# Both halves of each weight block kept in a DRAM scratch and loaded as one pair, two raw buffers, a one-function seed for the norms' reciprocal root

## The chip, the core and the metric

The kernel runs on one core of one Trainium2 chip. The metric is the device time of one execution in microseconds. The engines in the rows are PE (TensorE, matmuls), PEld (its weight loads), DVE (VectorE), ACT (ScalarE), POOL (GpSimd) and SP (SyncE), which here issues all DMAs.

## The reference

One block of a network: a state-space scan and a gated feed-forward, each behind a layer norm whose output is scaled and shifted by vectors made from a conditioning input. The input is (1, 2048, 1024) in fp32.

```python
mod = (silu(c) @ wmod).reshape(1, 6, 1, -1)        # sa, ca, ga, sb, cb, gb; ga and gb kept at least 0.25 from zero
h = layernorm(x) * (1 + ca) + sa
xp = h @ x_proj_w.T                                # 32 columns for dt, 16 for B, 16 for C
dt = softplus(xp[..., :32] @ dt_proj_w.T + dt_proj_b)
for t in range(2048):                              # 1024 channels x 16 states
    s = exp(dt[t] * A) * s + dt[t] * B[t] * h[t]
    y[t] = (s * C[t]).sum(states)
x = x + ga * (y + D * h)
h = layernorm(x) * (1 + cb) + sb
gate = h @ gate_w.T + (h @ gate_a.T) @ gate_b.T    # 1024 -> 2752, rank 16
up   = h @ up_w.T   + (h @ up_a.T) @ up_b.T
hidden = silu(gate) * up
out  = hidden @ down_w.T + (hidden @ down_a.T) @ down_b.T
return x + gb * out
```

## The kernel before

**Tiling.** Channels lie on the 128 partitions, tokens on the free axis. The 2048 tokens are cut into six chunks of 256, 320, 368, 368, 368 and 368 (`CH`). The feed-forward of one chunk is a *pass* of `NU` = 72 *units*: one `lora_a`, 44 `gate` and `up` units (25 matmuls each), three `lora_down` and 24 `down` units (21 or 24 matmuls each), in three parts of the hidden dimension. In the first two parts one more `gate` and `up` pair stands between the last hidden tile that `lora_down` needs and `lora_down` itself; in the third it follows directly on the last `up`. A unit needs one block of weights, of up to 128 x 1152 fp32.

**Split products.** Every fp32 product is made of three matmuls in the fast format fp32r: weight high x input high, weight high x input low, weight low x input high. So each block exists as a high half (`whi`, the rounded copy) and a low half (`wlo`, the difference).

**Where the halves come from.** Of 72 blocks, 48 (`PREP`) are prepared before the first pass, between the first scans: SP loads the raw block (`load_prep`), ACT rounds it (`hi_part`, L852, and L854 for the low-rank rows), POOL subtracts (L1267), and SP stores the low half to `lo_scratch` in DRAM (`store_prep`, L526). The high half is thrown away. The other 24 (`OTF`, every third unit) are done in the first pass (POOL L1297, `store_otf` L531). In every pass SP loads for each unit the raw block (`load_raw`, L550) and the low half (`load_lo`, L566), and ACT makes the high half again (`split_hi`, L990), two units ahead of PE. There are three buffers each for `raw`, `whi` and `wlo`: `load_raw(g + 4)` waits for the split of unit g + 1, and `load_lo(g + 3)` for the end of unit g on PE.

**What runs beside it.** During the pass of chunk c the scans of chunk c + 1 run, in 64 *groups* of two channel tiles and one state. For a group ACT makes the decays (exp, L831) and keeps the last state (`hst`, L848), DVE forms the input (L1053) and scans (L1168, two), POOL multiplies by C (L1284) and adds to y (L1257). Groups and the pieces of the norms are dealt out over the units by `pieces_at`, from weights in a table. Each engine has a queue in program order, and all walk through the same list of units: DVE and ACT take the results of unit g - 1 (`used`, `before`, `after`) between the pieces of units g and g + 1. A *head* norm opens the scans of a chunk, a *tail* norm (`TAIL_AT`) its feed-forward: squares are summed on PE, ACT computes a seed of the reciprocal root as exp(-0.5 ln(v)) (L890, L892, piece `rstd`), DVE sharpens it in four steps (L1118 to L1124), DVE multiplies (L1128), and ACT scales and shifts (L909, L910); POOL makes the low half `xlo` (L1275), for which `lora_a` waits.

**The end of the hidden loop.** `hhi` and `hlo` are the halves of the hidden tile: DVE L1191, ACT L1009, POOL L1305. `lora_down` waits for the last `hlo` of its part before its first matmul.

**SP at the start of a pass.** In program order: the last output store of the chunk before (L570), then `load_x` (L536, 1.47 MB), which waits until that chunk's outputs have landed, then the weight loads.

## Time and profile before

| | us |
|---|---|
| median of 3 runs (lowest, highest) | 2398.21 (2397.32, 2401.29) |
| profiled execution | 2402.57 |
| its span, first to last instruction | 2400.6 |
| preparation and scans of the first chunk, up to | 388 |
| passes, from one `lora_a` result to the next | 388 to 736, 1085, 1445, 1807, 2109, end |

The boundaries of the passes are the starts of the six instructions L997, which read the `lora_a` result (388.32, 736.32, 1085.54, 1445.08, 1806.87 and 2109.07 us). A matmul's record is longer than its turn on the engine, since matmuls are pipelined; the pace is read from starts. The profile's page gives over the whole span PE 87% busy, POOL 64%, DVE 60%, ACT 60%, and the DMA queue 68%. These are averages over stages with different limits, so the rows below go by stage. A row of the view by stage has the stretch, its length, busy us (instructions) of PE, PEld, DVE, ACT and POOL, the granted clock as a share of 2.4 GHz, the DMA share and GB/s. "issue" in a bracket stands for idle time for which the profile shows no releaser.

### The profile page before, as it was taken

To read this page: it belongs to the slowest core of one execution; us is meant where nothing else is said; L and a number is where in the kernel's file an instruction comes from. 1 tells how busy PE (TensorE), PEld (TensorE's weight loads), DVE (VectorE), ACT (ScalarE), POOL (GpSimd) and SP (SyncE) were. 2 spreads that over 40 slices of the span, in tenths; PEclk is the share of its full clock that TensorE was granted. 3 is DMA by queue.
4 is the path that set the end of the run, shared out by engine and by line. 5 is a ranking of instruction groups with operands and counts; after the bars stand their busy time and mean duration, and the time that the engine had idled before them with its cause. 6 is when DMAs were issued, how large, how long until landed. Compare 5 with 4: busy or idle time off the path is not lost.

```text
span 2400.6 us, 34580 instructions
## 1 busy us (share of the span) xinstructions
PE 2085.1 (87%) x11700; PEld 1888.9 (79%) x11700; DVE 1446.0 (60%) x2118; ACT 1430.1 (60%) x2798; POOL 1545.0 (64%) x960
## 2 busy tenths in 40 slices
PE   6587754877778989979999989999989999999999
PEld 3243334877767888868999978999979999999998
DVE  4665676767665688755778756678757775211111
ACT  3776766767655677665676655676656565532332
POOL 1576668988867876857876857876859897100000
PEclk9798877999889999989999999999999999999999
DMA  8777634666757677656666656666658777787785
GB/s 334 259 267 229 187 122 154 230 224 227 240 177 256 201 248 238 219 195 237 198 237 226 212 188 242 194 239 225 215 189 263 257 240 267 232 279 260 252 273 197
DMA packets 156032, 547.89 MB, mean 228 GB/s; under 512 B 17104, under 2 KB 29648, under 8 KB 152784
## 3 DMA queue, kind: packets, MB, share of 16 engines
q1 hardware_dynamic: 155856, 545.68, 68.0%
q8 instruction: 94, 1.54, 0.2%
q14 instruction: 82, 0.67, 0.1%
HBM read 498.32 MB, written 47.30 MB: 227 GB/s over the span
## 4 chain that ended last, share of the span: by engine, by line
PE 53%; DVE 16%; ACT 13%; issue 8%; POOL 5%; DMA 4%; SPq 0%; DVEq 0%; ACTq 0%; POOLq 0%
PE FP L762 43%; DVE ring L1168 7%; PE FP L650 4%; DVE ring L1053 3%; POOL ring L1284 2%; ACT SC L831 2%; PE FP L679 2%; ACT whi L990 2%; ACT sqb L950 2%; DVE FP L1143 1%; DMA raw<-w_gu 1%; POOL y L1257 1%; PE FP L786 1%; PE FP L624 1%; PE FP L628 1%
## 5 line engine op out<-in xcount | busy, mean ns | idle before, releaser
L1284 POOL TENSOR_TENSOR ring<-ring,c_row 128x736 f32<-128x736 f32 (+2 forms) x372 | 621.6, 1671 | 350.7 <-ACT hst L848 350.2
L762 PE MATMUL FP<-xhi,whi 128*128 128x368 f32 (+2 forms) x2160 | 713.0, 330 | 106.6 <-ACT dtb L955 27.3
L831 ACT ACTIVATE SC<-dtb,aneg 128x368 f32<-128x368 f32 (+2 forms) x768 | 409.3, 544 | 529.7 <-DVE ring L1168 525.2
L762 PE MATMUL FP<-xhi,wlo 128*128 128x368 f32 (+2 forms) x2160 | 703.7, 326 | 0.0
L762 PE MATMUL FP<-xlo,whi 128*128 128x368 f32 (+2 forms) x2160 | 703.6, 326 | 0.0
L1168 DVE TENSOR_TENSOR_SCAN ring<-SC,hst,ring 128x368 f32<-128x368 f32 (+1 forms) x640 | 579.7, 947 | 6.5 <-ACT SC L831 6.5
L1257 POOL TENSOR_TENSOR y<-y,ring 128x736 f32<-128x736 f32 (+1 forms) x320 | 555.0, 1734 | 13.7
L762 PEld LDWEIGHTS FP<-xhi,whi 128*128 128x128 f32 x2160 | 422.9, 196 | 120.7 <-ACT whi L990 66.0
L990 ACT ACTIVATE whi<-raw 128x1024 fp32r<-128x1024 f32 (+2 forms) x408 | 409.1, 1009 | 145.0 <-PE FP L786 69.7
L762 PE MATMUL FP<-hhi,whi 128*128 128x368 f32 (+5 forms) x1188 | 393.1, 331 | 66.2 <-POOL hlo L1305 46.6
L762 PEld LDWEIGHTS FP<-xlo,whi 128*128 128x128 f32 x2160 | 421.9, 195 | 1.1
L762 PEld LDWEIGHTS FP<-xhi,wlo 128*128 128x128 f32 x2160 | 421.6, 195 | 0.0
L762 PE MATMUL FP<-hlo,whi 128*128 128x368 f32 (+5 forms) x1188 | 388.0, 327 | 0.0
L762 PE MATMUL FP<-hhi,wlo 128*128 128x368 f32 (+5 forms) x1188 | 387.8, 326 | 0.0
L1053 DVE TENSOR_TENSOR ring<-hb,SC 128x736 f32<-128x736 f32 (+2 forms) x384 | 328.0, 854 | 94.9 <-PE FP L679 72.1
L1305 POOL TENSOR_TENSOR hlo<-hid,hhi 128x368 fp32r<-128x368 f32 (+2 forms) x132 | 122.6, 929 | 300.1 <-ACT hhi L1009 299.9
L762 PEld LDWEIGHTS FP<-hhi,whi 128*128 128x128 f32 (+1 forms) x1188 | 226.6, 191 | 75.6 <-issue 51.0
L1188 DVE SCALAR_TENSOR_TENSOR hid<-hid,FP 128x368 f32<-128x368 f32 (+2 forms) x132 | 67.3, 510 | 274.5 <-ACT hid L1002 273.2
L762 PEld LDWEIGHTS FP<-hlo,whi 128*128 128x128 f32 (+1 forms) x1188 | 227.0, 191 | 3.1 <-issue 0.2
L762 PEld LDWEIGHTS FP<-hhi,wlo 128*128 128x128 f32 (+1 forms) x1188 | 226.9, 191 | 2.8
L1207 DVE SCALAR_TENSOR_TENSOR y<-FP,mod,y 128x368 f32<-128x368 f32 (+2 forms) x144 | 81.7, 568 | 197.6 <-PE FP L762 197.3
L1267 POOL TENSOR_TENSOR wlo<-raw,whi 128x1152 fp32r<-128x1152 f32 (+4 forms) x48 | 116.8, 2434 | 89.7 <-ACT whi L854 57.2
(106 smaller groups left out, 2236.4 us busy)
## 6 DMA issues: line engine op xcount, KB each, us to landing
wlo<-lo_scratch SPq DMA_DIRECT2D x249, 576.0 KB, 4.4
raw<-w_gu SPq DMA_DIRECT2D x249, 512.0 KB, 5.0
raw<-w_dn SPq DMA_DIRECT2D x107, 448.0 KB, 4.1
wlo<-lo_scratch SPq DMA_DIRECT2D x91, 448.0 KB, 3.9
raw<-w_dn SPq DMA_DIRECT2D x53, 512.0 KB, 4.5
wlo<-lo_scratch SPq DMA_DIRECT2D x51, 512.0 KB, 4.0
raw<-w_gu SPq DMA_DIRECT2D x44, 576.0 KB, 4.7
lo_scratch<-wlo SPq DMA_DIRECT2D x44, 576.0 KB, 6.4
```

What stands on the lines that cost most here:

```text
L650: last = mm(bank, ones[:, :], of[:, i, 0:T], start=(i == 0), stop=(i == ND - 1))
L762: last = mm(out, w, x, start=(start and k == 0 and e == 0), stop=(stop and k == n - 1 and e == 2))
L831: A(decays(c, n, a), tile_of(dtb, c, i), ACT.Exp, scale=aneg[:, i * NS + s:i * NS + s + 1]).then_inc(a_da[a], 1)
L990: A(whi[:, s, 0:w], raw[:, r, 0:w], ACT.Copy).then_inc(a_hi, 1)
L1053: V.tensor_tensor(ring_of(c, n), pair_of(hb, c, q), over_pair(SC[:, BC0 + k % 2, 0:T]), ALU.mult).then_inc(v_dbx, 1)
L1168: V.tensor_tensor_scan(buf, decays(c, n, a), buf, hst[:, s * ND + i:s * ND + i + 1] if c else 0.0, ALU.mult, ALU.add).then_inc(v_scan[a], 1)
L1188: V.scalar_tensor_tensor(out=h, in0=h, scalar=1.0, in1=bank, op0=ALU.add, op1=ALU.mult).then_inc(v_used, 1)
L1207: V.scalar_tensor_tensor(out=y[:, c % 3, j, 0:T], in0=bank, scalar=modc(GB, j), in1=y[:, c % 3, j, 0:T], op0=ALU.mult, op1=ALU.add).then_i ...
L1257: G.tensor_tensor(ypair(c, q), ypair(c, q), ring_of(c, n), ALU.add).then_inc(g_add, 1)
L1267: G.tensor_tensor(wlo[:, s, 0:w], raw[:, i % RAW_SLOTS, 0:w], whi[:, s, 0:w].bitcast(F32), ALU.subtract).then_inc(g_prep, 1)
L1284: G.tensor_tensor(buf, buf, over_pair(c_of(k)), ALU.mult).then_inc(g_hc, 1)
L1305: G.tensor_tensor(hlo[:, k, 0:T], hid[:, j % 2, 0:T], hhi[:, k, 0:T].bitcast(F32), ALU.subtract).then_inc(g_hlo, 1)
```

## The change

All weights of a unit now lie in one tile `wts` with four slots, high and low half side by side, and `w_scratch` in DRAM keeps both. `store_prep` and `store_otf` store the pair; `load_pair` loads it from the scratch, for every unit but the 24 of the first pass that are split there. `split_hi` is left for these 24 alone. There are two raw buffers instead of three. The norm's seed is one activation, `Abs_reciprocal_sqrt`. `lora_down` waits for the last `hlo` before its last three matmuls only. The cut of the diff:

```diff
-RAW_SLOTS, HI_SLOTS, BANKS = 3, 3, 4
-AHEAD_HI, AHEAD_RAW = 2, 4
+W_SLOTS, RAW_SLOTS, BANKS = 4, 2, 4
+PREP_SLOTS = W_SLOTS
+AHEAD_HI = 2
...
-    lo_dram = nc.dram_tensor("lo_scratch", (NU, P, SLOT), F32, kind="Internal").ap()
+    w_dram = nc.dram_tensor("w_scratch", (NU, P, 2, SLOT), F32, kind="Internal").ap()
...
+        wts = sb("wts", [P, W_SLOTS, 2, SLOT], F32R)
         raw = sb("raw", [P, RAW_SLOTS, SLOT])
-        whi = sb("whi", [P, HI_SLOTS, SLOT], F32R)
-        wlo = sb("wlo", [P, HI_SLOTS, SLOT], F32R)
...
-                sp.dma_start(lo_dram[PREP[i], :, 0:w], wlo[:, i % HI_SLOTS, 0:w].bitcast(F32)).then_inc(d_kept[i % HI_SLOTS], 16)
+                sp.dma_start(w_dram[PREP[i], :, :, 0:w], wts[:, i % PREP_SLOTS, :, 0:w].bitcast(F32)).then_inc(d_kept[i % PREP_SLOTS], 16)
...
-            def load_raw(g):
+            def load_raw(k):
+                u = OTF[k]
...
-            def load_lo(g):
+            def load_pair(g):
...
+                if g == 0:
+                    preps_stored(sp)
+                if g >= W_SLOTS:
+                    sp.wait_ge(pe_unit, g - W_SLOTS + 1)
+                    if g - W_SLOTS in OTF:
+                        sp.wait_ge(d_kept_late, 16 * (OTF.index(g - W_SLOTS) + 1))
                 if c == 1 and u in OTF:
                     sp.wait_ge(d_kept_late, 16 * (OTF.index(u) + 1))
-                sp.dma_start(wlo[:, g % HI_SLOTS, 0:w].bitcast(F32), lo_dram[u, :, 0:w]).then_inc(d_lo[g % HI_SLOTS], 16)
+                sp.dma_start(wts[:, g % W_SLOTS, :, 0:w].bitcast(F32), w_dram[u, :, :, 0:w]).then_inc(d_w[g % W_SLOTS], 16)
...
                     if kind == "lora_down":
-                        pe.wait_ge(g_hlo, c * NH + k1)
+                        pe.wait_ge(g_hlo, c * NH + k1 - 1)
...
                     products(out, pairs[:-1], stop=False)
+                    if kind == "lora_down":
+                        pe.wait_ge(g_hlo, c * NH + k1)
...
             def prep_hi(i):
                 act.wait_ge(d_prep[i % RAW_SLOTS], 16 * (i // RAW_SLOTS + 1))
-                if i >= HI_SLOTS:
-                    prep_ready(act, i - HI_SLOTS)
+                if i >= PREP_SLOTS:
+                    act.wait_ge(d_kept[i % PREP_SLOTS], 16 * (i // PREP_SLOTS))
...
-                    A(row, bank_of("sq", k, c), ACT.Ln, scale=1.0 / D, bias=epsc).then_inc(a_ln, 1)
-                    act.wait_ge(a_ln, li + 1)
-                    A(row, row, ACT.Exp, scale=-0.5).then_inc(a_rs, 1)
+                    A(row, bank_of("sq", k, c), ACT.Abs_reciprocal_sqrt, scale=1.0 / D, bias=epsc).then_inc(a_rs, 1)
...
-                    if g + AHEAD_HI < CHUNKS * NU:
+                    if g + AHEAD_HI in OTF:
                         split_hi(g + AHEAD_HI)
...
             def lo_in_pass(u):
-                s, w = u % HI_SLOTS, lo_cols(u)
-                pool.wait_ge(a_hi, u + 1)
-                if u >= HI_SLOTS:
-                    pool.wait_ge(pe_unit, u - HI_SLOTS + 1)
-                    if u - HI_SLOTS in OTF:
-                        pool.wait_ge(d_kept_late, 16 * (OTF.index(u - HI_SLOTS) + 1))
+                s, w, k = u % W_SLOTS, lo_cols(u), OTF.index(u)
+                pool.wait_ge(a_hi, k + 1)
```

SP, the DMA queue, from the last loads of the preparation into the first pass. `raw` loads are L550 before and L548 now, scratch loads L566 and L563, stores in the pass L534. Before:

```order
L550 DMA raw<-w_la 128x1024 [waits prep_lo_ready]
L550 DMA raw<-w_gu 128x1152 [waits prep_lo_ready]
L550 DMA raw<-w_gu 128x1024 [waits prep_lo_ready]
L550 DMA raw<-w_gu 128x1024 [waits weight_hi_ready]
L566 DMA wlo<-lo_scratch 128x1024 [waits lo_stored2,lo_stored1,lo_stored0]
L566 DMA wlo<-lo_scratch 128x1152
L550 DMA raw<-w_gu 128x1152 [waits pass_lo_ready,weight_hi_ready]
L566 DMA wlo<-lo_scratch 128x1152 [waits unit_done]
```

Now:

```order
L548 DMA raw<-w_gu 128x1152 [waits prep_lo_ready]
L548 DMA raw<-w_gu 128x1152
L563 DMA wts<-w_scratch 128x2x1024 [waits prep_stored2,prep_stored3,prep_stored1,prep_stored0]
L563 DMA wts<-w_scratch 128x2304 x2
L534 DMA w_scratch<-wts 128x2304 [waits pass_lo_ready]
L548 DMA raw<-w_gu 128x1152 [waits pass_lo_ready]
L563 DMA wts<-w_scratch 128x2304 [waits stored_in_pass,unit_done]
L563 DMA wts<-w_scratch 128x2304 [waits unit_done]
```

The four pair loads no longer stand behind a raw load that waits for ACT's split (`weight_hi_ready`), and a pair load in the first pass now waits for a store (`stored_in_pass`).

ACT in the pass of the third chunk, at the head norm of the fifth (1147 us in the trace), where a hidden tile (`hhi`), a group's turn, the seed and a tanh (`hid`) follow each other. L831, L848, L1002 and L1009 before are L830, L847, L995 and L1002 now. Before:

```order
L990 ACTIVATE whi<-raw 128x1024 [waits unit_done,raw_loaded1]
L1009 ACTIVATE hhi<-hid 128x368 [waits unit_used]
L831 ACTIVATE SC<-dtb,aneg 128x368 [waits scan0_done]
L831 ACTIVATE SC<-dtb,aneg 128x368 [waits scan1_done]
L848 ACTIVATE hst<-ring 128x2 [waits scan1_done,scan0_done]
L890 ACT_TABLE_LOAD [waits rstd_step]
L890 ACTIVATE seed<-FP,consts 128x368 [waits squares_summed]
L892 ACT_TABLE_LOAD
L892 ACTIVATE seed<-seed 128x368 [waits log_ready]
L1002 ACTIVATE hid<-FP 128x368 [waits hidden_lo_ready,unit_done]
L990 ACTIVATE whi<-raw 128x1024 [waits unit_done,raw_loaded2]
```

Now:

```order
L1002 ACTIVATE hhi<-hid 128x368 [waits unit_used]
L830 ACTIVATE SC<-dtb,aneg 128x368 [waits scan0_done]
L830 ACTIVATE SC<-dtb,aneg 128x368 [waits scan1_done]
L847 ACTIVATE hst<-ring 128x2 [waits scan1_done,scan0_done]
L889 ACT_TABLE_LOAD [waits rstd_step]
L889 ACTIVATE seed<-FP,consts 128x368 [waits squares_summed]
L995 ACT_TABLE_LOAD [waits hidden_lo_ready]
L995 ACTIVATE hid<-FP 128x368 [waits unit_done]
L840 ACTIVATE c_row<-SC 128x368 [waits state_c_ready,c_ready]
```

The copies `whi<-raw` are gone from between the decays, and the second table load stands behind the seed, ahead of the next tanh, with that tanh's own wait for PE behind it.

## Rows read from the trace of the kernel before

**Rows 1.** Busy time of PE, PEld, DVE, ACT, POOL, by stage (passes from 388 on).

```profile
57.00:378.00 321.00, 211.37 (x663) 102.58 (x663) 206.19 (x375) 233.32 (x555) 222.09 (x134) 0.79 0.60 200
388.00:736.00 348.00, 272.81 (x1859) 257.98 (x1859) 235.82 (x351) 230.29 (x466) 295.06 (x189) 0.89 0.67 220
736.00:1085.00 349.00, 303.22 (x1837) 287.62 (x1836) 247.36 (x339) 228.24 (x440) 258.75 (x160) 0.94 0.68 226
1085.00:1445.00 360.00, 333.42 (x1850) 317.42 (x1850) 250.97 (x339) 230.19 (x439) 257.66 (x158) 0.97 0.65 217
1445.00:1807.00 362.00, 333.47 (x1848) 317.59 (x1847) 248.49 (x336) 228.84 (x437) 259.97 (x159) 0.96 0.65 217
1807.00:2109.00 302.00, 302.00 (x1775) 296.93 (x1774) 184.32 (x241) 168.31 (x308) 211.96 (x131) 1.00 0.76 253
2109.00:2400.00 291.00, 285.86 (x1695) 283.68 (x1693) 41.32 (x74) 88.07 (x115) 21.64 (x22) 0.99 0.75 252
```

**Rows 2.** Groups of instructions: count, busy us, mean ns, idle before with releasers.

```profile
L762 PE MATMUL FP<-xhi,whi 128*128 128x368 f32 (+2 forms) x2160 | 713.0, 330 | 106.6 <-ACT dtb L955 27.3 <-issue 25.2 <-ACT whi L990 23.2
L762 PE MATMUL FP<-hhi,whi 128*128 128x368 f32 (+5 forms) x1188 | 393.1, 331 | 66.2 <-POOL hlo L1305 46.6 <-issue 10.4 <-ACT whi L990 8.6
L990 ACT ACTIVATE whi<-raw 128x1024 fp32r<-128x1024 f32 (+2 forms) x408 | 409.1, 1009 | 145.0 <-PE FP L786 69.7 <-PE FP L762 64.1 <-DMA raw<-w_gu 11.0
```

**Rows 3.** Timeline of PE: start us, us, instruction, [idle before it].

```profile
382.96 0.55 PE L762 MATMUL FP<-xhi,whi 128*128 128x256 f32 x1 [11.73 <-DMA wlo<-lo_scratch]
749.65 0.60 PE L762 MATMUL FP<-xhi,whi 128*128 128x320 f32 x1 [6.85 <-ACT whi L990]
1392.39 0.56 PE L762 MATMUL FP<-hhi,whi 128*80 128x368 f32 x1 [8.52 <-POOL hlo L1305]
1440.75 0.41 PE L762 MATMUL FP<-xhi,whi 128*128 128x368 f32 x1 [3.23 <-POOL xlo L1275]
1458.55 0.65 PE L762 MATMUL FP<-xhi,whi 128*128 128x368 f32 x1 [4.96 <-ACT whi L990]
```

**Rows 4.** Chain that ended last (start us, us, what), around 1445.

```profile
1392.39 3.63 PE FP L762 x11
1446.70 10.36 DMA raw<-w_gu
1458.55 6.37 PE FP L762 x24
1465.25 4.00 PE FP L762 x24
```

**Rows 5.** Group of DVE's first step after the seed.

```profile
L1118 DVE TENSOR_SCALAR FP<-FP 128x368 f32<-128x368 f32 (+2 forms) x12 | 6.3, 521 | 45.7 <-ACT seed L892 45.7
```

**Rows 6.** Timeline of ACT at one norm.

```profile
1415.22 1.28 ACT L892 ACT_TABLE_LOAD   x1
1416.52 0.51 ACT L892 ACTIVATE seed<-seed 128x368 f32<-128x368 f32 x1
```

**Rows 7.** DMA issues: KB each, median us to landing.

```profile
raw<-w_gu SPq DMA_DIRECT2D x44, 576.0 KB, 4.7
lo_scratch<-wlo SPq DMA_DIRECT2D x44, 576.0 KB, 6.4
```

**Rows 8.** Busy time in 20 us of the preparation.

```profile
100.00:120.00 20.00, 14.88 (x44) 6.78 (x44) 10.83 (x21) 15.60 (x40) 17.51 (x11) 0.74 0.90 345
```

**Rows 9.** DMA rate from 98 to 122 us, in 40 slices.

```profile
GB/s 297 259 344 419 418 469 430 422 434 425 423 410 413 400 429 408 417 392 412 431 426 435 439 436 442 242 68 55 55 105 36 305 405 440 399 162 113 84 305 439
```

**Rows 10.** Timelines of SP and ACT: a block's store round, and the next-but-one split.

```profile
84.72 0.33 SPq L521 DMA_DIRECT2D raw<-w_gu  x1
88.67 1.05 ACT L852 ACTIVATE whi<-raw 128x1024 fp32r<-128x1024 f32 x1
```

**Rows 11.** Timelines of PE and POOL in the first pass.

```profile
502.07 0.55 PE L762 MATMUL FP<-hhi,whi 128*128 128x256 f32 x1 [5.31 <-issue]
499.89 2.07 POOL L1297 TENSOR_TENSOR wlo<-raw,whi 128x896 fp32r<-128x896 f32 x1
```

More of the change, by code:

```diff
@@ L196, in period_pieces @@
     return [(p, w or weight(p)) for p, w in out]
-OTF = [u for u in range(NU) if u % HI_SLOTS == 1]
+OTF = [u for u in range(NU) if u % 3 == 1]
 PREP = [u for u in range(NU) if u not in OTF]
@@ L439, in group_after, with loads_until, preps_stored @@
             return (c + 1, 0) if c + 1 < CHUNKS else None
-        def lo_loads(g):
-            s = g % HI_SLOTS
-            return len([k for k in range(s, g + 1, HI_SLOTS) if k >= NU or k not in OTF])
+        def loads_until(g):
+            return len([k for k in range(g % W_SLOTS, g + 1, W_SLOTS) if k not in OTF])
+        def preps_stored(engine):
+            for s in range(PREP_SLOTS):
+                engine.wait_ge(d_kept[s], 16 * len(range(s, NPREP, PREP_SLOTS)))
         def ypair(c, q):
@@ L530, in store_otf @@
                 sp.wait_ge(g_lo, OTF.index(u) + 1)
-                sp.dma_start(lo_dram[u, :, 0:w], wlo[:, u % HI_SLOTS, 0:w].bitcast(F32)).then_inc(d_kept_late, 16)
+                sp.dma_start(w_dram[u, :, :, 0:w], wts[:, u % W_SLOTS, :, 0:w].bitcast(F32)).then_inc(d_kept_late, 16)
             def load_x(c):
@@ L593, in _ @@
                     store_prep(p[1])
-            for g in range(AHEAD_RAW):
-                load_raw(g)
-            for g in range(HI_SLOTS):
-                load_lo(g)
+            for k in range(RAW_SLOTS):
+                load_raw(k)
+            for g in range(W_SLOTS):
+                load_pair(g)
             for g in range(CHUNKS * NU):
@@ L767, in unit @@
                 g, T = c * NU + u, CH[c]
-                s, bank = g % HI_SLOTS, BANK["unit", c, u]
-                hi, lo = whi[:, s, :], wlo[:, s, :]
+                s, bank = g % W_SLOTS, BANK["unit", c, u]
+                hi, lo = wts[:, s, 0, :], wts[:, s, 1, :]
                 k0, k1 = PARTS[part]
-                pe.wait_ge(a_hi, g + 1)
-                if c == 0 and u in OTF:
-                    pe.wait_ge(g_lo, OTF.index(u) + 1)
+                if g in OTF:
+                    pe.wait_ge(a_hi, OTF.index(g) + 1)
+                    pe.wait_ge(g_lo, OTF.index(g) + 1)
                 else:
-                    pe.wait_ge(d_lo[s], 16 * lo_loads(g))
+                    pe.wait_ge(d_w[s], 16 * loads_until(g))
                 bank_free(pe, "unit", c, u)
@@ L979, in split_hi @@
             def split_hi(g):
-                c, u = divmod(g, NU)
-                s, r, w = g % HI_SLOTS, g % RAW_SLOTS, raw_cols(u)
-                act.wait_ge(d_raw[r], 16 * (g // RAW_SLOTS + 1))
-                if g >= HI_SLOTS:
-                    act.wait_ge(pe_unit, g - HI_SLOTS + 1)
-                else:
-                    preps_done(act)
-                if c == 0 and u in OTF:
-                    hi_part(u, s, r).then_inc(a_hi, 1)
-                else:
-                    A(whi[:, s, 0:w], raw[:, r, 0:w], ACT.Copy).then_inc(a_hi, 1)
+                k = OTF.index(g)
+                act.wait_ge(d_raw[k % RAW_SLOTS], 16 * (k // RAW_SLOTS + 1))
+                if g >= W_SLOTS:
+                    act.wait_ge(pe_unit, g - W_SLOTS + 1)
+                else:
+                    preps_stored(act)
+                hi_part(g, wts[:, g % W_SLOTS, 0, :], raw[:, k % RAW_SLOTS, :]).then_inc(a_hi, 1)
             def before(c, u):
@@ L1219, in _ @@
                 V.memset(consts[:, 1 + f:2 + f], FACTORS[f][0])
-            for s in range(HI_SLOTS):
-                V.memset(whi[:, s, ND * P:].bitcast(F32), 0.0)
+            for s in range(PREP_SLOTS):
+                V.memset(wts[:, s, 0, ND * P:].bitcast(F32), 0.0)
             V.memset(small[:, 1, :], 0.0).then_inc(v_const, 1)
@@ L1288, in lo_in_pass @@
             def lo_in_pass(u):
[L1289 to L1297 removed]
+                s, w, k = u % W_SLOTS, lo_cols(u), OTF.index(u)
+                pool.wait_ge(a_hi, k + 1)
+                G.tensor_tensor(wts[:, s, 1, 0:w], raw[:, k % RAW_SLOTS, 0:w], wts[:, s, 0, 0:w].bitcast(F32), ALU.subtract).then_inc(g_lo, 1)
             def after(c, u):
```

60 lines of the change are left out of this document (22 added, 38 removed).

## The prediction

> **What bounds the kernel now.** I read the view by stage first. The kernel has three regimes. In the last two passes (1807 to 2400 us) PE is busy all the time at full clock and nothing else matters: 302 us for 1775 matmuls is 0.170 us each at 368 columns [rows 1]. In the four passes from 388 to 1807 no engine is full. PE is idle for 348 - 273 = 75, 46, 27 and 29 us of them and runs at a mean granted clock of 0.89, 0.94, 0.97 and 0.96 [rows 1]. Set against the pace of the full pass, the third needs 1850 x 0.170 = 315 us and takes 360; the second, at 320 columns, needs about 1837 x 0.148 = 272 and takes 349; the first about 1859 x 0.118 = 220 and takes 348, but there POOL is busy for 295 us, since it also makes the low halves of 24 blocks. POOL's 258 us and DVE's 250 are the floors of the others [rows 1]. Before 388, the preparation (57 to 378) has ACT at 233 of 321 us, POOL at 222, DMA at 0.60 [rows 1]. So there are some 45 + 45 + 75 + 50 us above the floors of the four mixed passes, and the question is how many of these hang on what is changed.
>
> Then the PE groups: what ended PE's idle time. For the units behind `xhi`: dtb (the keeping of dt by ACT) 27 us, "issue" 25, `whi` of L990 23; behind `hhi`: POOL's `hlo` 47, whi 9 [rows 2]. The timeline shows the single gaps: 11.7 us before the first `lora_a`, 6.9 and 5.0 us for `whi` a few units into a pass, 8.5 us for `hlo` at the last `lora_down`, 3.2 us for `xlo` before the next `lora_a` [rows 3]. A gap costs more than itself. Behind the one of 5.0 us a unit's 24 matmuls take 6.37 us and behind the one of 8.5 us 6.91, against 4.00 at full clock [rows 4]; the granted clock is at its lower level (1.2 GHz) there, which is what the 0.97 of the pass is made of. I price the clock at 2 us behind each gap over 3 us.
>
> **The change part by part.**
>
> *ACT's copies go.* All 408 instructions of L990, 409 us of ACT's time [rows 2], disappear, 72 us in each of the passes 1 to 5 (the count of a pass's units by 1.0 us). In the last pass ACT waits on PE before most of them, so they are worth nothing there. In the mixed passes PE's waits that end in whi are 23 + 9 = 32 us [rows 2], and three of them stand at the start of a pass: 6.9 us, 5.0 us [rows 3], and one of 3.0 like them. Their cause is SP, not ACT alone. SP sends the last outputs, waits for them, sends the 1.47 MB of `load_x` and only then the raw block of unit 4, which lands 10.4 us after its issue at 1446.7 [rows 4]. The pair load of unit 4 now stands at the same place in SP's queue, three units (12.6 us) ahead of its use, with the pairs of units 1 to 3 loaded already, and no copy behind it. The old load landed at 1457.1. The pair is 1152 KB instead of 512, at the DMA's 420 GB/s [rows 9] 1.6 us more; but the low half of unit 3 no longer shares the queue with it. PE gets there at about 1457. So of 15 us and 3 x 2 us of clock I take 15 and keep 6 for a late pair. Bounds: 0 and 21.
>
> The rest of ACT's share in the mixed passes is 17 us of whi, 27 of dtb, and the "issue" gaps of 25 + 10 us [rows 2], most of which lie in the first pass and are POOL's low half: PE starts at 502.07 when POOL ends L1297, begun at 499.89 after a group's product [rows 11]. ACT's 1.0 us copies stand between the decays, the tanh and the keeping of states, so all of these shorten, but only the whi ones vanish; POOL's work in the first pass stays. I take two fifths: 32 of 79. Bounds 5 and 70.
>
> *lora_down.* Of the last `lora_down`'s 24 matmuls, 21 now run inside the wait for `hlo`. It was 8.5 us [rows 3], so the 3.5 us of 21 matmuls at full clock fit (4.00 for 24 [rows 4]). Before, the unit took 6.9 us after the wait [rows 4]; now three matmuls are left (under 1 us), and what follows starts at low clock instead. I take 4.5 us in each mixed pass and 3 in the last: 21 us. Bounds 10 (only 2 us a pass) and 28. Behind it on PE wait the squares' sums of the tail norm, and DVE and ACT with them, so it is on the path.
>
> *The seed.* DVE's first step waits 45.7 us in 12 norms for it [rows 5]. The second function and its table load, 1.28 + 0.51 us [rows 6], leave the path: 1.8 us a norm. The number of table loads stays 25, since the next exp or tanh needs its own; but as the order shows that load stands ahead of an instruction that waits for a scan or for PE, so it lies in an idle time of ACT. At the tail norms this feeds `xlo`, for which PE waits 3.2 us [rows 3] in three passes, and three or four copies leave the same stretch of ACT. 4 us in each, 12 in all (bounds 3 and 16). The head norms I count at nothing (the scans go on beside them). At the first softplus a table load that was not there stands in the path: 1 us of loss.
> The Trainium skill (ScalarE: Activation LUTs, What ACT_TABLE_LOAD costs) gives about 2.66 us for a switch, 1.28 of load and 1.38 of drain. The trace does not agree: the next instruction starts 0.02 us behind the load [rows 6]. By the page's figure the tail norms would give 5 us each instead of 4, the sum 3 us more.
>
> *The start of the passes.* The first `lora_a` waits 11.7 us [rows 3], its low half being issued only when SP has passed a raw load that waits for ACT's split. The pairs now go out before. But its input is itself finished only a few us earlier, so 3 us.
>
> *What is added.* (a) In the preparation each of 48 stores is twice as large and there are two raw buffers. The raw load of block i + 2 is issued when POOL is done with block i, and ACT wants it when it comes to block i + 2: 84.72 and 88.67 us in the worst common case [rows 10], 4.0 us, where a load takes 4.7 and a store 6.4 at the median [rows 7]. Of the 44 blocks from 57 us on, I find 9 with less than 6 us between the two (1.6 to 5.5), short by 20 us together against 6.3. DMA is at 0.90 and 345 GB/s in the busiest 20 us [rows 8], where some five stores of 0.59 MB more would ask for 490; the rate when it has a backlog is 420 [rows 9], so there is a spill of a few us. Behind a waiting ACT stand the decays, so DVE and POOL wait too. I take 10 us, bounds 0 and 60 (1.4 us at every block).
> (b) In the first pass `load_pair(g + 4)` waits for the store of unit g's pair, issued as unit g begins: 6.4 us for half of it [rows 7], so some 8 to 9, and SP's whole queue stands behind it. The pair then lands about 14 us after unit g began; PE reaches g + 4 after 4 x 348/72 = 19 us. 3 us for the places where PE is faster, bounds 0 and 15.
> (c) Bytes: a gate or up pair has 1152 KB where raw and low half had 1088; the last pass would go from a share of 0.75 to 0.79. Nothing.
> The Trainium skill (DMA: Bandwidth & Descriptors, Bandwidth) holds that between HBM and SBUF some 358 GB/s per core bind, not the 435 of the fabric. The rows do not bear it out: 22 slices of 0.6 us in a row stand at 392 to 469 [rows 9]. By the page's limit (a) would be about 10 us dearer.
>
> **Sum.** 15 + 32 + 21 + 12 + 3 = 83 us, and 7 us of clock behind the dtb and hlo gaps of 2 to 4 us that shorten, makes 90 gained; 10 + 3 + 1 = 14 lost; net 76. From the profiled execution's 2402.6 (span 2400.6) that is 2326.6. It lies 4.4 us above the median of 2398.2, by which I go: 2322.
>
> **The rivals.**
> *The scans keep the pace.* DVE, ACT and POOL hand a group round (ACT's decay waits for DVE's scan, POOL for ACT's `hst`), and PE, once through a gap, meets the next wait of the same chain. Then only the lora_down at its lower bound, the pass starts and the first `lora_a` count: 15 + 10 + 3 - 14 = 14 us, 2384. For: DVE, ACT and POOL all wait for each other though none is above 0.75 in the second to fourth pass. Against: PE is at 0.9 there [rows 1], so little can be taken back before PE is full.
> *ACT was the knot.* Every mixed pass falls to near its floor: first 315, second 295, third and fourth 322: 33 + 54 + 38 + 40 = 165, and 3 at the end, less 14: 2244. For: ACT sits in every chain of a group. Against: POOL's 295 us in the first pass leave it little room.
> *Slower.* The preparation becomes bound by its two raw buffers. A buffer is loaded, split by ACT (1.35 us), subtracted by POOL (2.6) and waits in their queues between (some 3 us); with two of them a block takes half of that and of the load. If loads land after 10.4 us, as one does behind a large transfer [rows 4], that is (10.4 + 7) / 2 = 8.7 us a block against 5.7 now: 44 x 3.0 = 132 us lost instead of 10, so 2398 - 90 + 132 + 4 = 2444. It outweighs the gain from a landing of about 8.3 us on. Against: 4.7 at the median [rows 7].
> *The pairs come late.* PE waits for DMA in all passes where it waited for ACT. A pair needs 1.18 MB at 420 GB/s = 2.8 us of a unit's 4.2, so only backlog could do it; at half a us for each of 88 gate and up units of the last two passes and half the gain lost before, 2398 - 45 + 14 + 44 = 2411.
>
> **How the numbers follow.** Forecast's case 0.52, scans keep the pace 0.20, ACT the knot 0.15, slower 0.08, late pairs 0.05. Predicted 2322 us. The forecast's own bounds are about 2290 to 2365; the range 2255 to 2388 takes in the first rival and most of the second. 0.2% (5 us) is about what a measurement of this kernel can tell from no change. Faster by more than that: 0.52 + 0.20 + 0.15 less a little, 0.86; slower: 0.08 and a part of the late pairs, 0.09; same 0.05.
>
> **What would show it.** Passes of about 330, 325, 342 and 342 us, the last two at 300 and 288. No PE wait ended by `wts` from ACT outside the first pass. The gap at the last `lora_down` in two parts, the wait itself at about 5 us before three matmuls. ACT busy near 1020 us. DVE's wait for the seed at 25 us instead of 45.7. ACT waiting for raw blocks in the preparation, 10 us in total, and the first `lora_a` at about 388. Wrong if the preparation ends past 410, if the mixed passes stay above 345, or if PE's gaps are ended by DMA.

## The result and the profile after

| | before | after |
|---|---|---|
| median of the runs beside each other, us | 2399.16 (2397.32 to 2401.29) | 2329.75 (2327.44 to 2337.13) |
| ratio, 95% interval | | 0.9715 (0.9695 to 0.9734) |
| span of the profiled execution, us | 2400.6 | 2325.6 |
| first pass begins at | 388.3 | 387.6 |
| the six passes, us | 348.0, 349.2, 359.5, 361.8, 302.2, 291.5 | 346.0, 323.3, 338.9, 341.1, 302.2, 286.6 |

The kernel is 69 us faster, 2322 was forecast. The profiled spans differ by 75 us: 0.7 before the first pass, 2.0 in it, then 25.9, 20.6 and 20.7, nothing in the fifth and 4.9 in the last. Where 348 us became 346, nearly the whole change did nothing; that is the main question behind the result.

The view by stage of the kernel after, with the columns of [rows 1]:

```profile
57.00:378.00 321.00, 212.32 (x653) 102.74 (x651) 205.46 (x374) 229.13 (x545) 216.20 (x131) 0.78 0.78 288
387.60:733.50 345.90, 274.32 (x1867) 259.45 (x1866) 235.82 (x351) 185.96 (x415) 297.73 (x191) 0.88 0.75 265
733.50:1056.80 323.30, 294.46 (x1831) 280.55 (x1830) 246.75 (x339) 164.02 (x368) 258.91 (x160) 0.97 0.71 251
1056.80:1395.70 338.90, 325.30 (x1848) 312.03 (x1847) 251.11 (x339) 165.84 (x366) 258.06 (x158) 0.99 0.69 239
1395.70:1736.80 341.10, 327.26 (x1847) 313.76 (x1846) 248.61 (x336) 164.69 (x363) 259.70 (x159) 0.98 0.69 238
1736.80:2039.00 302.20, 302.20 (x1776) 297.13 (x1775) 184.22 (x241) 102.70 (x235) 211.84 (x131) 1.00 0.76 260
2039.00:2325.60 286.60, 283.57 (x1694) 282.05 (x1692) 41.32 (x74) 24.00 (x47) 21.59 (x22) 1.00 0.77 266
```

In the second to fourth pass PE's idle time went from 46, 27 and 29 us to 29, 14 and 14, and its granted clock from 0.94, 0.97 and 0.96 to 0.97, 0.99 and 0.98. DVE and POOL are busy as long as before, within 0.7 us, ACT 64 us less a pass. In the first pass the granted clock (0.88) and PE's idle time (72 us, 75 before) are nearly what they were.

PE's timeline, the gaps that answer to [rows 3]:

```profile
382.91 0.55 PE L759 MATMUL FP<-xhi,wts 128*128 128x256 f32 x1 [7.73 <-POOL xlo L1267]
746.69 0.41 PE L759 MATMUL FP<-xhi,wts 128*128 128x320 f32 x1 [3.44 <-DMA wts<-w_scratch]
1349.29 0.60 PE L759 MATMUL FP<-hhi,wts 128*80 128x368 f32 x1 [4.92 <-POOL hlo L1291]
1391.36 0.41 PE L759 MATMUL FP<-xhi,wts 128*128 128x368 f32 x1 [2.29 <-POOL xlo L1267]
1410.16 0.43 PE L759 MATMUL FP<-xhi,wts 128*128 128x368 f32 x1 [1.58 <-DMA wts<-w_scratch]
```

In order, the wait of 11.7 us became 7.7 and now ends with the input; 6.85 became 3.4; 8.52 became 4.9; 3.23 became 2.3; 4.96 became 1.6. The releaser of the second and fifth is now a transfer, no longer ACT. The chain behind the third, first the unit in the kernel before (it waited for `hlo` and then did all its 24 matmuls), then the kernel now, where three are left:

```profile
1392.39 6.91 PE FP L762 x24
```

```profile
1348.28 0.97 POOL hlo L1291
1349.25 0.04 issue
1349.29 1.21 PE FP L759 x3
```

The norm's seed, ACT's timeline, and DVE's group that waits for it [rows 5, 6]:

```profile
1364.56 1.28 ACT L889 ACT_TABLE_LOAD   x1
1365.85 0.57 ACT L889 ACTIVATE seed<-FP,consts 128x368 f32<-128x368 f32 x1
1366.43 1.28 ACT L830 ACT_TABLE_LOAD   x1
1371.14 0.57 ACT L830 ACTIVATE SC<-dtb,aneg 128x368 f32<-128x368 f32 x1 [3.42 <-DVE ring L1162]
```

```profile
L1112 DVE TENSOR_SCALAR FP<-FP 128x368 f32<-128x368 f32 (+2 forms) x12 | 6.2, 520 | 24.0 <-ACT seed L889 24.0
```

The wait is 24.0 us where it was 45.7, 1.8 us for each of 12 norms. The second load stands behind the seed, in front of the next decay; that decay waits for DVE's scan for another 3.42 us after the load, so the load costs nothing here. In the preparation ACT now waits for raw blocks, 15.3 us between 57 and 340 us, none there before. First these waits of ACT (us in total, times, longest), then the DMA issues (KB, median us to landing):

```profile
ACT wts L851 <- DMA raw<-w_gu: 7.4, 7, 3.2
ACT wts L851 <- DMA raw<-w_dn: 4.0, 2, 2.2
ACT wts L851 <- DMA raw<-w_td: 3.9, 1, 3.9
```

```profile
wts<-w_scratch SPq DMA_DIRECT2D x249, 1152.0 KB, 5.3
w_scratch<-wts SPq DMA_DIRECT2D x44, 1152.0 KB, 7.4
raw<-w_gu SPq DMA_DIRECT2D x44, 576.0 KB, 6.3
```

### The profile page after: what moved, and what is told of

Same layout as the page of the kernel before. It is cut to its first block, busy times and chain, and to the rows that moved or that the text cites. A ratio compares the mean times of both kernels' runs of the same rounds, so it can differ in the third digit from the quotient of the medians.

```text
span 2325.6 us, 33254 instructions
## 1 busy us (share of the span) xinstructions
PE 2064.8 (89%) x11700; PEld 1875.5 (81%) x11700; DVE 1444.6 (62%) x2119; ACT 1061.0 (46%) x2378; POOL 1543.6 (66%) x960
## 4 chain that ended last, share of the span: by engine, by line
PE 59%; DVE 14%; ACT 8%; issue 8%; POOL 6%; DMA 3%; DVEq 0%; ACTq 0%; SPq 0%; POOLq 0%
PE FP L759 50%; DVE ring L1162 6%; PE FP L647 4%; DVE ring L1047 3%; POOL ring L1276 2%; DVE FP L1137 2%; ACT SC L830 1%; ACT sqb L947 1%; PE FP L783 1%; DMA raw<-w_gu 1%; PE FP L720 1%; PE FP L676 1%; POOL y L1251 1%; DMA wts<-w_scratch 1%; POOL xlo L1267 1%
## 5 line engine op out<-in xcount | busy, mean ns | idle before, releaser
L759 PE MATMUL FP<-xhi,wts 128*128 128x368 f32 (+2 forms) x4320 | 1079.3, 326 | 76.8 <-issue 28.0
L759 PEld LDWEIGHTS FP<-xhi,wts 128*128 128x128 f32 x4320 | 774.8, 194 | 86.8 <-issue 78.3
L830 ACT ACTIVATE SC<-dtb,aneg 128x368 f32<-128x368 f32 (+2 forms) x768 | 412.1, 545 | 730.7 <-DVE ring L1162 729.5
L759 PE MATMUL FP<-xlo,wts 128*128 128x368 f32 (+2 forms) x2160 | 700.4, 324 | 0.0
L759 PE MATMUL FP<-hhi,wts 128*128 128x368 f32 (+5 forms) x2376 | 574.3, 323 | 39.8 <-POOL hlo L1291 22.9
L759 PEld LDWEIGHTS FP<-hhi,wts 128*128 128x128 f32 (+1 forms) x2376 | 410.5, 187 | 47.0 <-POOL hlo L1291 23.6
L759 PEld LDWEIGHTS FP<-xlo,wts 128*128 128x128 f32 x2160 | 419.3, 194 | 1.1
L759 PE MATMUL FP<-hlo,wts 128*128 128x368 f32 (+5 forms) x1188 | 381.4, 321 | 0.0
L1182 DVE SCALAR_TENSOR_TENSOR hid<-hid,FP 128x368 f32<-128x368 f32 (+2 forms) x132 | 67.2, 509 | 253.8 <-ACT hid L995 252.5
L759 PEld LDWEIGHTS FP<-hlo,wts 128*128 128x128 f32 (+1 forms) x1188 | 222.4, 187 | 2.1 <-issue 0.2
L1259 POOL TENSOR_TENSOR wts<-raw,wts 128x1152 fp32r<-128x1152 f32 (+4 forms) x48 | 116.3, 2423 | 94.7 <-ACT wts L853 57.8
L1185 DVE SCALAR_TENSOR_TENSOR hid<-hid,FP 128x368 f32<-128x368 f32 (+2 forms) x132 | 67.3, 510 | 159.9 <-PE FP L783 153.8
L995 ACT ACTIVATE hid<-FP 128x368 f32<-128x368 f32 (+2 forms) x132 | 58.0, 439 | 147.0 <-PE FP L783 146.9
L1002 ACT ACTIVATE hhi<-hid 128x368 fp32r<-128x368 f32 (+2 forms) x132 | 63.1, 478 | 120.4 <-DVE hid L1185 119.9
```

The costliest lines, as they stand in the source:

```text
L759: last = mm(out, w, x, start=(start and k == 0 and e == 0), stop=(stop and k == n - 1 and e == 2))
L830: A(decays(c, n, a), tile_of(dtb, c, i), ACT.Exp, scale=aneg[:, i * NS + s:i * NS + s + 1]).then_inc(a_da[a], 1)
L1185: V.scalar_tensor_tensor(out=h, in0=h, scalar=0.5, in1=bank, op0=ALU.mult, op1=ALU.mult).then_inc(v_used, 1)
L1259: G.tensor_tensor(wts[:, s, 1, 0:w], raw[:, i % RAW_SLOTS, 0:w], wts[:, s, 0, 0:w].bitcast(F32), ALU.subtract).then_inc(g_prep, 1)
```

## Why the first pass stayed: its waits before and after

PE's waits in the first pass, of the kernel before:

```profile
PE FP L762 <- issue: 35.6, 12, 5.3
PE FP L762 <- POOL hlo L1305: 11.0, 2, 10.5
PE FP L762 <- ACT dtb L955: 10.8, 6, 4.1
PE FP L762 <- ACT whi L990: 9.5, 3, 5.4
```

And of the kernel after:

```profile
PE FP L759 <- issue: 44.9, 12, 5.8
PE FP L759 <- ACT dtb L952: 10.8, 4, 4.4
PE FP L759 <- POOL hlo L1291: 7.8, 2, 7.3
```

The 9.5 us of waits for ACT's copies are gone and the "issue" gaps are 9.3 us longer. [rows 11] shows one of these ending 0.1 us behind POOL's low half; in the kernel after all 12 do. So nearly the same time is waited for under another name. POOL is busy 297.7 of 345.9 us there. Three experiments take that cause away, move it, or make it smaller.

In every experiment the passes are given as differences from the kernel after, in us. A second profile of the kernel after, taken on another chip, has 346.0, 323.3, 338.9, 341.4, 302.2 and 286.6, so the same kernel repeats its passes to 0.3 us. But a pass also depends on what went before it: PE's wait for a pair near the start of the second pass, 3.4 us above, was 2.1 in that second profile and between 1.4 and 6.8 in the six experiments below that leave SP's queue and the four slots as they are. In the next experiment the second pass moves by 5 us that way. So a difference of one pass by up to 5 us is not by itself the effect of an edit; a gap that changed with it is better evidence. The start of the first pass can't be read closely either: nine executions with the same code up to there began it between 384.1 and 392.7, 387.0 in the middle. An edit above a line moves its number, so the lines in the rows of an experiment are a few off those of the kernel after.

**The low halves of the first pass left out** (only 8 columns of each of the 24 blocks are made there):

```diff
+                w = 8
                 G.tensor_tensor(wts[:, s, 1, 0:w], raw[:, k % RAW_SLOTS, 0:w], wts[:, s, 0, 0:w].bitcast(F32), ALU.subtract).then_inc(g_lo, 1)
```

> The changed kernel with POOL's subtraction for the 24 blocks of the first pass cut to 8 columns (so their low halves are left out there; the result is not the reference's). It takes some 55 us of POOL's work out of the first pass. Theory (the first pass, 346 us with POOL busy for 298, is bound by POOL, and PE's gaps without a releaser are its waits for these low halves): the pass falls to 300 to 315 us, the total to about 2290. Rival (the first pass is bound by something else in the list of units, as DVE or SP's wait for the stores): it stays above 335 us, total 2320.

Measured: 2297.17 us, ratio 0.9572 (0.9550 to 0.9594). The first pass changed by -37.9; the second and third, whose code is the same, by +5.1 and +2.2. The stage of the first pass, and PE's wait for a pair at the start of the second:

```profile
385.10:693.20 308.10, 259.90 (x1857) 243.64 (x1856) 234.82 (x351) 185.98 (x416) 244.75 (x189) 0.94 0.81 287
```

```profile
710.69 0.63 PE L759 MATMUL FP<-xhi,wts 128*128 128x320 f32 x1 [6.83 <-DMA wts<-w_scratch]
```

53 us less of POOL are 38 us less of pass, and the clock rises from 0.88 to 0.94; 7 of the 38 are given back in the next two passes. The total is 33 us below the kernel after. POOL sets the first pass while it makes the low halves.

**The same work on DVE.** `lo_in_pass` is moved from POOL's program to DVE's, at the same place, ahead of the pieces of the unit before:

```diff
-                G.tensor_tensor(wts[:, s, 1, 0:w], raw[:, k % RAW_SLOTS, 0:w], wts[:, s, 0, 0:w].bitcast(F32), ALU.subtract).then_inc(g_lo, 1)
...
+                V.tensor_tensor(wts[:, s, 1, 0:w], raw[:, k % RAW_SLOTS, 0:w], wts[:, s, 0, 0:w].bitcast(F32), ALU.subtract).then_inc(g_lo, 1)
```

> The changed kernel with the 24 low halves of the first pass made by DVE instead of POOL, at the same place in the list of units. With the subtraction cut away the first pass took 308 us. Theory (POOL was its bound, DVE has 110 us idle there): a block takes 1.3 us on DVE against 2.4 on POOL, the pass takes 312 to 325 us, the total is 2300 to 2310. Rival (DVE is in every group's chain too, and stands in front of the scans): the pass stays above 335 us.

Measured: 2341.08 us, ratio 0.9743 (0.9729 to 0.9758); first pass +6.7, the next three +3.2, +2.3 and -3.0. The expectation of a first pass of 312 to 325 us was wrong by 28 to 41. The stage, and DVE's group (busy, mean ns, idle before it with what ended it):

```profile
391.50:744.20 352.70, 271.36 (x1837) 252.59 (x1836) 272.85 (x374) 186.87 (x416) 266.05 (x168) 0.88 0.72 253
```

```profile
L1207 DVE TENSOR_TENSOR wts<-raw,wts 128x1152 fp32r<-128x1152 f32 (+3 forms) x24 | 41.2, 1717 | 36.2 <-ACT wts L853 24.9 <-ACT wts L851 11.1
```

DVE needs 1.72 us a block where POOL needs 2.44 (means of the same 24). But it stands idle for 36 us before the 24 subtractions, because ACT's split isn't done when the unit begins, and the scans stand behind it in DVE's queue. No engine is above 273 of 352.7 us. The reading that fits is that a wait put in front of the scans costs what a full engine would; the same subtractions behind the scans of a unit were not tried.

**Fewer blocks split in the pass** (16 instead of 24, so 56 in the preparation; this kernel also has the later `load_x` of the last section):

```diff
-OTF = [u for u in range(NU) if u % 3 == 1]
+OTF = [u for u in range(NU) if u % 9 in (1, 4)]
```

> As x_mid, and only 16 blocks instead of 24 are split in the first pass, the other 8 in the preparation. Theory (POOL is the bound of the first pass, and of the preparation nobody is): the pass loses 8 x 2.4 us of POOL and falls from 346 to about 328 us, the preparation grows by less, 5 to 12 us; in all 6 to 12 us less than x_mid. Rival (in the preparation each block costs its 1.4 us on ACT and 2.6 on POOL in the one chain): it grows by 20 us or more, and the total is the same or longer.

Measured: 2326.96 us, ratio 0.9698 (0.9685 to 0.9711); first pass -20.7, its start 18 us later than in the kernel that differs by nothing else (392.7). The expectation was 6 to 12 us less than that kernel (2321.79); it came out 5 us longer, which is the rival's outcome.

```profile
57.00:410.00 353.00, 225.72 (x676) 110.48 (x675) 208.40 (x377) 245.26 (x571) 244.69 (x145) 0.74 0.82 301
410.60:735.90 325.30, 261.30 (x1850) 247.35 (x1849) 235.28 (x351) 177.36 (x403) 279.79 (x184) 0.92 0.74 268
```

The pass gives, the preparation takes: some 2.2 us a block there against 2.6 here. The low halves' cost can be moved but not dropped.

## The parts taken one by one

**The two-step seed put back.**

```diff
-                    A(row, bank_of("sq", k, c), ACT.Abs_reciprocal_sqrt, scale=1.0 / D, bias=epsc).then_inc(a_rs, 1)
+                    A(row, bank_of("sq", k, c), ACT.Ln, scale=1.0 / D, bias=epsc).then_inc(a_ln, 1)
+                    act.wait_ge(a_ln, li + 1)
+                    A(row, row, ACT.Exp, scale=-0.5).then_inc(a_rs, 1)
```

> The changed kernel with the seed made by ln and exp again, nothing else. Theory (the tail norm's chain feeds xlo, for which PE waits): 1.8 us more at each of the five tail norms of passes 0 to 4 and one in the preparation, so 6 to 10 us more in all, 2338, the PE gap before lora_a 1.8 us longer in passes 1 to 3, the head norms without effect. Rival (the second table load, now ahead of the next exp or tanh, costs as much as it saved): 0 to 2 us, 2330. Second rival (head norms count too, since DVE waits in each): 1.8 x 11 = 20 us, 2350.

Measured: 2335.38 us, ratio 0.9723 (0.9701 to 0.9745). Passes -2.8, +8.1, +2.4, +0.4, 0, 0: 8 us together, of 12 in the sum. The time itself is 6 us above the median after and 10 above the second one, with intervals that overlap. The expected sign was a wait of PE for `xlo` that is 1.8 us longer in three passes. It came at the end of the second pass alone, where the kernel after has 3.57 us:

```profile
1058.10 0.65 PE L759 MATMUL FP<-xhi,wts 128*128 128x368 f32 x1 [5.36 <-POOL xlo L1269]
```

The next two stayed at 2.3 and 2.4 us. So the seed is shown on PE's path in one of three passes; how much of the 8 us is its doing stays open.

**`lora_down` waits for `hlo` before its first matmul again.**

```diff
-                        pe.wait_ge(g_hlo, c * NH + k1 - 1)
+                        pe.wait_ge(g_hlo, c * NH + k1)
```

> The changed kernel with lora_down waiting for its last hidden tile before its first matmul again, nothing else. Theory: 4 to 5 us more in each of the passes 0 to 3 and 3 in the last, 20 us, 2350; the wait for hlo in the third part 8 us instead of 4.9. Rival (what follows on PE has to wait for ACT and DVE anyway, the gap only moves): 5 us or less, 2335.

Measured: 2346.75 us, ratio 0.9777 (0.9753 to 0.9801). Passes +0.4, +6.6, +3.3, +3.9, 0, +2.9: 17 us. PE's timeline has the old wait again:

```profile
1352.82 0.56 PE L759 MATMUL FP<-hhi,wts 128*80 128x368 f32 x1 [8.50 <-POOL hlo L1289]
```

That is 4.6 us in each of three mixed passes and 3 in the last, as costed; 1.6 us of the second pass's share is a longer wait for a pair (5.0 where 3.4 was). In the first pass the wait for `hlo` grew by 3.2 us (7.3 to 10.6) and the pass by 0.4, since POOL is the limit there.

**ACT's copies put back as dead weight.** In every pass from the second on, ACT copies as many columns as `split_hi` did, inside `raw`, at its place in the queue and with its wait for PE; nobody reads the result.

```diff
                     if g + AHEAD_HI in OTF:
                         split_hi(g + AHEAD_HI)
+                    elif NU <= g + AHEAD_HI < CHUNKS * NU:
+                        act.wait_ge(pe_unit, g)
...
+                        A(raw[:, 0, 0:raw_cols((g + AHEAD_HI) % NU)], raw[:, 1, 0:raw_cols((g + AHEAD_HI) % NU)], ACT.Copy).then_inc(a_more, 1)
```

> The changed kernel with ACT's copies put back as dead weight: in passes 1 to 5, where a unit's high half was rounded before, ACT copies one raw buffer into the other (1.0 us, same shape, same wait for PE), and nobody waits for the result. It does work that the kernel does not need. Theory A (ACT's time itself was on the chains of the groups and of xlo): half or more of what passes 1 to 3 gained comes back, 30 to 45 of 67 us, 2365. Theory B (what counted was that PE waited for the copy and its raw block, not ACT's time): passes 1 to 3 stay within 3 us each of 323, 339 and 341, total under 2340.

Measured: 2339.47 us, ratio 0.9745 (0.9724 to 0.9766). Passes +1.1, +3.8, +2.9, +2.9, 0, 0. The third pass:

```profile
1058.30:1400.10 341.80, 326.35 (x1852) 312.34 (x1851) 250.87 (x339) 229.88 (x438) 259.19 (x158) 0.99 0.69 237
```

ACT is at 229.9 us again, as in [rows 1], and the pass is 2.9 us longer, not 20. So little of the gain came from ACT's time as such: it is worth about 10 us in three passes.

**The same, with PE waiting for the dead copy** before each unit:

```diff
+                if g >= NU:
+                    pe.wait_ge(a_more, g - NU + 1)
```

> As act_back, and PE in passes 1 to 5 waits for the dead copy of its own unit before the unit, as it waited for the high half before. The copy reads no new data, so no transfer is added. act_back gave back about 10 us in passes 1 to 3 (347, 327, 342, 344 us for the first four passes, against 346, 323, 339, 341). Theory (the dependency of PE on ACT's queue was the cost: ACT comes to the copy late, behind group turns and norms): passes 1 to 3 rise by 8 us each or more over act_back, total 2365. Rival (the cost was the raw loads and SP's order, with three buffers, and ACT's queue came late only because its raw block did): less than 3 us each, total under 2348.

Measured: 2347.35 us, ratio 0.9773 (0.9758 to 0.9787). Beyond the dead weight, passes +6.9, +3.5 and -0.3: 10 us for the dependence. The total fits the rival's bound (2348), the second pass neither reading.

**The two small edits alone on the kernel before.** It keeps its raw loads, three buffers and 408 copies, and has the one-function seed and the late wait of `lora_down`:

```diff
-                        pe.wait_ge(g_hlo, c * NH + k1)
+                        pe.wait_ge(g_hlo, c * NH + k1 - 1)
...
+                    if kind == "lora_down":
+                        pe.wait_ge(g_hlo, c * NH + k1)
...
-                    A(row, bank_of("sq", k, c), ACT.Ln, scale=1.0 / D, bias=epsc).then_inc(a_ln, 1)
-                    act.wait_ge(a_ln, li + 1)
-                    A(row, row, ACT.Exp, scale=-0.5).then_inc(a_rs, 1)
+                    A(row, bank_of("sq", k, c), ACT.Abs_reciprocal_sqrt, scale=1.0 / D, bias=epsc).then_inc(a_rs, 1)
```

> The kernel before with the two small edits alone (lora_down waits before its last three matmuls, one-function seed); the weights are split and loaded as before. Theory (the three parts add up): 15 to 20 us below the kernel before, 2383, so that the pairs alone are worth some 50 us. Rival (in the old kernel PE meets the next wait for a high half, so the small parts only count with the pairs): 5 us or less, 2395.

Measured: 2359.15 us, ratio 0.9835 (0.9821 to 0.9849): 40 us of the 69 with two edits of a few lines. I had expected half of that. Against the kernel before, the passes differ by -1.2, -12.0, -7.5, -10.7, 0 and -4.9 (36 us), and the first begins 8 us earlier (379.9), about as much as that start varies; taken out of the kernel after, the same two edits cost 8 + 17 = 25 in the passes. Next to the dead-weight kernel whose PE waits for ACT, the passes two to four are 3.2, 6.8 and 7.5 longer: 18 us. The two differ in the raw loads with the copies' wait for them, in SP's order at the start of a pass, and in the number of buffers. PE's timeline in the kernel with the two edits alone:

```profile
739.25 0.61 PE L762 MATMUL FP<-xhi,whi 128*128 128x320 f32 x1 [6.77 <-ACT whi L990]
1429.90 0.65 PE L762 MATMUL FP<-xhi,whi 128*128 128x368 f32 x1 [6.07 <-ACT whi L990]
```

In the chain that ended last, what stands ahead of the second gap is the raw block's transfer:

```profile
1417.91 10.48 DMA raw<-w_gu
1428.39 0.02 issue
1428.42 1.06 ACT whi L990
```

At the same places the kernel whose PE waits for the dead copies has 2.08 and 1.23 us, ended by a DMA. So ACT's time is not what those gaps were made of; the late raw block was.

## The queue at the start of a pass, and the buffers

**Three slots for pairs, three raw buffers** (and the waits that follow from three slots):

```diff
-W_SLOTS, RAW_SLOTS, BANKS = 4, 2, 4
+W_SLOTS, RAW_SLOTS, BANKS = 3, 3, 4
```

> The changed kernel with three slots for the pairs and three raw buffers. Two readings. The preparation: with two raw buffers ACT waited 15 us there for raw blocks and block 48 was split at 337.0 us against 330.8 before; theory: with three it waits for under 3 us and block 48 comes at about 331; rival (the doubled stores hold DMA up, not the number of buffers): it stays at 335 or later. The passes: pairs are then loaded two units ahead instead of three, 8.4 us for a landing of 5.3; theory: passes 2 to 5 within 2 us of 339, 341, 302 and 287; rival (a pass's start, where SP is held for 10 us): 3 to 5 us more in passes 1 to 3.

Measured: 2342.70 us, ratio 0.9752 (0.9738 to 0.9767). ACT waits for no raw block between 57 and 340 us (for stores it waits 7 us), the last 128x1024 split of the preparation begins at 330.78, as before the change, and not at 336.95, and the first pass at 382.2. That is 5 us below the middle of the nine with two buffers, and below each of them. Passes +0.4, +4.5, +5.7, +10.5, 0, +2.0; PE's timeline shows what the fourth slot did:

```profile
1070.14 0.67 PE L759 MATMUL FP<-xhi,wts 128*128 128x368 f32 x1 [5.28 <-DMA wts<-w_scratch]
1416.18 0.68 PE L759 MATMUL FP<-xhi,wts 128*128 128x368 f32 x1 [6.76 <-DMA wts<-w_scratch]
```

The gaps at the start of a pass are back at their old size, with a DMA as releaser. Loading pairs doesn't remove them; loading them one unit earlier takes them down to 3.4, nothing and 1.6. The fourth slot is worth 23 us in the passes.

**`load_x` moved from unit 0 to unit 4** of a pass:

```diff
                 if u == 0 and c:
                     store_out(c - 1, ND - 1)
-                    if c + 2 < CHUNKS:
-                        load_x(c + 2)
+                if u == 4 and c and c + 2 < CHUNKS:
+                    load_x(c + 2)
```

> The changed kernel with the load of the next x put four units later in SP's queue, so that the pair loads of a pass's start no longer stand behind the wait for the outputs. Theory (PE's gaps that end in a pair's landing, 3.4 us in pass 1 and 1.6 in pass 2, are this): they vanish, passes 1 to 3 are 2 to 4 us shorter together with the clock, in total 4 to 8 us, 2323. Rival (the wait only moves to unit 4, where it blocks the pairs of units 8 and 9): no change.

Measured: 2348.22 us, ratio 0.9776 (0.9760 to 0.9793). Passes 0, +4.6, +8.6, +7.7: 21 us longer, where the expectation was 4 to 8 less and the rival no change. The pair's gap is gone, and in each of the three passes a larger one stands a little further on, where PE sums the new x:

```profile
752.99 0.98 PE L647 MATMUL FP<-y,ones 128*128 128x368 f32 x1 [6.55 <-DMA y<-x_t]
1083.15 1.60 PE L647 MATMUL FP<-y,ones 128*128 128x368 f32 x2 [5.05 <-DMA y<-x_t]
1430.98 1.59 PE L647 MATMUL FP<-y,ones 128*128 128x368 f32 x2 [5.45 <-DMA y<-x_t]
```

**`load_x` at unit 1**, beside the kernel after once more:

```diff
                 if u == 0 and c:
                     store_out(c - 1, ND - 1)
-                    if c + 2 < CHUNKS:
-                        load_x(c + 2)
+                if u == 1 and c and c + 2 < CHUNKS:
+                    load_x(c + 2)
```

> The changed kernel itself, as the measure for the runs beside it on one chip. Expected: 0.9715 of the time before within 0.003. If it comes out at 0.974 or above, the passes 1 to 3 of its first trace (323, 339, 341 us) were on the short side, and what the single undone parts gave back is to be counted from this run.

> The changed kernel with the load of the next x one unit later in SP's queue, behind the pair of unit 4. Four units later was too late: PE waited 5 us for x. Theory: the waits for a pair at the start of passes 1 and 2 (3.4 and 1.6 us) vanish and x still comes in time, since its use is some 26 us into the pass; 3 to 6 us less than the changed kernel beside it. Rival (the pair of unit 5 is late instead): within 2 us.

Measured: the kernel after again 2325.76 us, ratio 0.9694 (0.9679 to 0.9709); with `load_x` one unit later 2321.79, ratio 0.9676 (0.9663 to 0.9689). In the passes two to four it differs from that second profile by -3.9, 0 and -2.8, PE's gaps for pairs (2.08 and 2.48 us there) are gone and none for x has come. It is the fastest version run that computes the whole result, but the intervals of the two overlap. The kernel with 16 blocks has the same later load, no gap for a pair at the start of a pass either, and passes two to four at -3.5, 0 and +0.3 against the same profile. So the gaps are shown to go, and 3 to 7 us with them are likely and not shown.

## Why the prediction came out as it did

The mechanism was right in the second to fourth pass and wrong in the first, and the total is within 8 us. The spans fell by 75, where the sum has 76. That agreement is in part luck: it is better than its terms were, since several misses cancelled. Two of the prediction's own signs of being wrong came: a mixed pass above 345 us (the first) and gaps of PE ended by DMA (two, 5.0 us together).

- *The first pass: the step that failed.* The prediction named POOL's 295 us as its limit and then still forecast 330, taking two fifths of all waits including the "issue" ones, and 4.5 us of `lora_down`. It is 346. With a limit there, a wait removed comes back under another name (9.5 us of `whi`, 9.3 more of "issue"). The list of passes was also inconsistent with the sum: 388 and the six add up to 2315, ten less than the sum's span.
- *Start of the passes:* 15 costed, 18 measured in three passes, by the two kernels that differ in loads and buffers. Moving one load in SP's queue moves these gaps, so SP's queue is a cause, as said; what solved most of it was the fourth slot, which the prediction only mentions as "three units ahead".
- *The rest of ACT's copies:* 32 costed; dead weight 10 and dependence 10 make 20 in the second to fourth pass. PE's waits for dtb in the second to fourth pass, which the sum counted in, went only from 17.0 us (10 times) to 14.6 (8 times), while the 22.3 us for `whi` went altogether.
- *lora_down:* 21 costed, 17 measured, and the wait of 4.9 us before three matmuls is the one forecast (about 5). The unit's 6.91 us, which the prediction quotes from [rows 4], is the whole of what is cut off there at 3.63. The granted clock over it was 0.57. *Seed:* 12 costed, 4 for each of three tail norms; 8 measured, with PE's wait for `xlo` longer in one of them only; DVE's wait 24.0 (25 forecast). *First lora_a:* 3 costed; the time from the end of `xlo` to it fell from 4.1 to 0.15 us.
- *What is added:* (a) 10 costed. ACT waits 15.3 us for raw blocks, but the kernel with the old preparation and the new seed begins its passes at 379.9 and the one with three raw buffers at 382.2, against 387.0: 5 us for the two raw buffers, 7 for these and the doubled stores, each from one execution and beside a spread of 8, so neither is shown. (b) 3 costed: no gap of PE in the first pass is ended by a DMA. (c) the last pass's share is 0.77, not 0.79, and costs nothing.
- *What made up for the misses:* the two small edits are worth 36 us in the passes of the old kernel and 25 in the new one. Step by step from before to after (small edits, loads and buffers, dependence, ACT's time), and with the first pass in, the passes fall by 36 + 17 + 10 + 11 = 74 us, which is all; with the small edits at their price in the new kernel it is 63. So 11 us belong to either, as a wait that one part closes is no longer there for the other. Which of the waits these are was not separated.
- *ACT busy* was forecast at 1020 and is 1061.0, from 1430.1. The 409.1 us are the busy time of the copies by themselves; their records overlap those of their neighbours on ACT, and without the copies ACT's busy time before is 1072.8, only 357 us less. The other 12 went with the seed's second function and what else changed.
- *The rivals.* "The scans keep the pace" is not what happened (it needed 2384), but its pattern, the next wait of the same chain, is what the first pass shows. The kernel with dead copies shows that little hung on ACT alone, which speaks against "ACT was the knot". "Slower by the preparation" was decided by the landing of raw loads: 6.2 us at the median in the preparation, from 4.9 before, below the 8.3 from which it would have decided. "Late pairs" are the two gaps of 3.4 and 1.6 us now, and gaps of 5 to 7 us with three slots.

## What to carry to other kernels

Where one engine is near its limit in a stage, take nothing for waits that other engines end there; first ask what the next wait in line is. Price an edit by the gap that it closes and not by the busy time that it removes: 364 us of ACT's copies put back cost 11 us, while one more slot and a wait moved by 21 matmuls cost no engine time and gave 23 and 17. And an in-order DMA queue is a schedule of its own: `load_x` at unit 0 delays the weights, at unit 4 it is late itself. Last, before one pass is compared with another, look at a pass whose code did not change: here it moved by up to 5 us.
